# An attention and quantised-linear block on one core: the order of one DMA queue in seven units, the opening tiles, and a few moves beside them

## The reference

```python
xn = (x - mean) / sqrt(var + 1e-5)
# attention: 16 query heads, 8 key/value heads (two query heads share one), head size 16
q, k, v = xn @ Wq.T, xn @ Wk.T, xn @ Wv.T
energy = q @ k.T - abs(i - j) * 2.0 ** -(head + 1)          # ALiBi
att = softmax(energy / sqrt(16)) @ v
attention = att @ Wo.T + bo
# linear: xn quantised per token to int8, int8 weights
x_scale = max(max(abs(xn)), 1e-6) / 127
linear = (round(xn / x_scale) @ weight_q.T) * x_scale * weight_scale + bias
```

## Time and profile before

| | |
|---|---|
| median of three runs | 1568.98 us |
| profiled execution, its own time | 1568.38 us |
| its span, first to last instruction | 1566.4 us |
| granted TensorE clock, mean | 0.992 |
| TensorE matmuls busy | 1497.0 us, 96% |
| VectorE busy | 1394.6 us, 89% |
| ScalarE busy | 1184.8 us, 76% |
| GpSimd busy | 1076.1 us, 69% |
| DMA engines, share over the span on the main queue | 34.2% |

### The profile page before, as it was taken

How to read it: one execution, slowest core, us unless ns; L and a number is a source line. 1 busy time by engine, 2 the same in 40 slices (tenths; PEclk the granted TensorE clock), 3 DMA queues, 4 the chain that set the end, 5 groups by cost and what they waited for, 6 DMA issues and landing times.

```text
span 1566.4 us, 42517 instructions
## 1 busy us (share of the span) xinstructions
PE 1497.0 (96%) x16284; PEld 583.0 (37%) x16284; DVE 1394.6 (89%) x1698; ACT 1184.8 (76%) x2331; POOL 1076.1 (69%) x1627
## 2 busy tenths in 40 slices
PE   5899999999999999999989999999999999999998
PEld 5333333333333333333333334333333333333333
DVE  5999989999899998999979999899998988999981
ACT  3467777777787776887767887777877777788885
POOL 5467777777788876787757877677877776533332
PEclk9999999999999999999999999999999999999999
DMA  6522243333334334333333433433333332312212
GB/s 169 140 76 71 74 100 81 93 98 81 105 83 108 96 79 109 91 92 101 84 92 94 105 85 91 103 98 96 97 83 96 94 92 65 82 49 68 72 44 62
DMA packets 197291, 140.98 MB, mean 90 GB/s; under 512 B 107040, under 2 KB 165728, under 8 KB 197088
## 3 DMA queue, kind: packets, MB, share of 16 engines
q1 hardware_dynamic: 197088, 138.27, 34.2%
HBM read 81.40 MB, written 35.63 MB: 75 GB/s over the span
## 4 chain that ended last, share of the span: by engine, by line
PE 47%; DVE 30%; SPq 9%; issue 8%; DMA 3%; POOL 2%; ACT 0%; POOLq 0%; DVEq 0%; ACTq 0%
DVE row_max L999 27%; PE ps_ring L1279 15%; PE ps_pv L1355 13%; PE ps_row L1296 9%; PE ps_ring L1395 4%; PE ps_ring L1415 3%; SPq L464 2%; SPq L468 2%; SPq L506 2%; DMA q<-neg_max_t 1%; SPq L472 1%; PE ps_ring L1398 1%; DMA k<-k_alibi 1%; DVE pv_turned L1039 1%; PE ps_ring L1409 1%
## 5 line engine op out<-in xcount | busy, mean ns | idle before, releaser
L999 DVE TENSOR_REDUCE row_max<-ps_row 128x1 f32<-128x1024 f32 x1024 | 1199.5, 1213 | 114.7 <-PE ps_row L1298 99.4
L1171 ACT ACTIVATE probs<-ps_ring 128x512 f32<-128x512 f32 x2048 | 1084.5, 601 | 245.2 <-PE ps_ring L1279 242.6
L1279 PE MATMUL ps_ring<-q,k 122*32 122x512 bf16 x8192 | 636.6, 383 | 19.9 <-DMA q<-neg_max_t 19.0
L762 POOL TENSOR_TENSOR probs<-probs,near 128x256 f32<-128x256 f32 x512 | 375.2, 733 | 324.8 <-ACT probs L1171 318.9
L1355 PE MATMUL ps_pv<-probs,v_unit 128*32 128x512 f32 x4096 | 533.5, 596 | 0.0
L1279 PEld LDWEIGHTS ps_ring<-q,k 122*32 122x32 bf16 x8192 | 215.1, 95 | 518.0 <-ACT probs L1171 324.7
L1296 PE MATMUL ps_row<-k,q 64*128 64x512 bf16 x944 | 326.2, 385 | 25.8 <-DVE row_max L999 11.4
L1298 PE MATMUL ps_row<-k_again,q_again 64*128 64x512 bf16 x944 | 326.0, 385 | 0.0
L1296 PEld LDWEIGHTS ps_row<-k,q 64*128 64x128 bf16 x944 | 84.2, 93 | 320.3 <-issue 199.6
L1355 PEld LDWEIGHTS ps_pv<-probs,v_unit 128*32 128x32 f32 x4096 | 124.7, 110 | 54.2 <-issue 7.7
L1298 PEld LDWEIGHTS ps_row<-k_again,q_again 64*128 64x128 bf16 x944 | 84.0, 92 | 0.0
(11 more groups left out here) (84 smaller groups left out, 1012.0 us busy)
## 6 DMA issues: line engine op xcount, KB each, us to landing
parts_dram<-parts SPq DMA_DIRECT2D x59, 288.0 KB, 3.0
q_again<-q SPq DMA_DIRECT2D x63, 256.0 KB, 3.3
token_b<-token_dram SPq DMA_DIRECT2D x53, 256.0 KB, 4.1
q<-parts_dram SPq DMA_DIRECT2D x128, 96.0 KB
k<-parts_dram SPq DMA_DIRECT2D x256, 32.0 KB
q<-parts_dram SPq DMA_DIRECT2D x128, 64.0 KB
att_dram<-att_unit SPq DMA_DIRECT2D x126, 64.0 KB
att_t<-att_dram SPq DMA_DIRECT2D x56, 128.0 KB, 2.9
```

The source lines that it names most:

```text
L762: pool.tensor_tensor(here, here, near[:, u % KV_HEADS, :].rearrange("p (e n) -> p e n", e=GROUP), ALU.mult).then_inc(weighted, 1)
L999: dve.tensor_reduce(row_max[:, par, e, qb:qb + 1], ps_row[qb % 2][:, :], AX_X, ALU.max, negate=True).then_inc(row_max_found, 1)
L1171: act.activation(probs[:, c % PBUFS, e, h * HALF:(h + 1) * HALF], ring_bank(u, c, e, h), ACT.Exp, scale=SCALE).then_inc(ring_freed, 1)
L1279: mm = pe.matmul(to[at, :], weights[:, at], moving, start=start, stop=stop)
```

## The change

On the queue, in the seven units u = 6, 14, ..., 54 (where set u + 2 is late), load_token, place_max, store_att and load_att_t move from the end of the unit's program to its start, the first before and the others behind load_again(u + 2), and so ahead of next_set(u + 3). In the opening stage tiles 0 to 7 are taken through on all engines before tiles 8 to 10, and the largest values of the first eight are found behind their last rest. In units 0 and 1 VectorE's tile work is split over blocks 1 and 3. In even units find_rsum, norm and turn_back change places. The projections of the last sequence are grouped in pairs.

```diff
@@ sync, unit(u, f)
-                if u + 2 < UNITS and late_set(u + 2):
+                copied = u + 2 < UNITS and late_set(u + 2)
+                if copied:
+                    if f["token"]:
+                        load_token(u + 1 + PREP_AHEAD)
                     load_again(u + 2, (u + 2) % SETS)
+                    place_max(u + 1, (u + 1) % SETS)
+                    store_att(u - 1)
+                    for t in f["next_att"]:
+                        load_att_t(t, t % 2)
                 if f["row_set"] and not late_set(u + 3):
                     next_set(u + 3)
...
-                if f["token"]:
-                    load_token(u + 1 + PREP_AHEAD)
-                if not f["last"]:
-                    place_max(u + 1, (u + 1) % SETS)
-                if f["prev"] and u % PAIR == 0:
-                    store_att(u - 1)
-                for t in f["next_att"]:
-                    load_att_t(t, t % 2)
+                if not copied:
+                    if f["token"]:
+                        load_token(u + 1 + PREP_AHEAD)
+                    if not f["last"]:
+                        place_max(u + 1, (u + 1) % SETS)
+                    if f["prev"] and u % PAIR == 0:
+                        store_att(u - 1)
+                    for t in f["next_att"]:
+                        load_att_t(t, t % 2)
@@ gpsimd, opening
-            for t in range(PREP_AHEAD):
-                if t + 4 < PREP_AHEAD:
+            for t in range(BLOCKS):
+                if t + 4 < BLOCKS:
                     find_rstd(t + 4, t % 2)
+                find_low(t, t % 2)
+            for t in range(BLOCKS, PREP_AHEAD):
+                find_rstd(t, t % 2)
+            for t in range(BLOCKS, PREP_AHEAD):
                 find_low(t, t % 2)
@@ gpsimd, unit(u, f)
+                    if c == 4 and f["prev"] and u % PAIR == 0:
+                        norm(u - 1)
                     if c == 4:
                         for made in f["made"][:1]:
                             weigh_linear(made)
...
-                    if c == 3 and f["prev"] and u % PAIR == 0:
-                        norm(u - 1)
@@ vector, opening
             first_stats(2)
-            find_first_largest(0)
             first_stats(3)
-            find_first_largest(1)
-            for t in range(PREP_AHEAD):
-                if t + 2 < PREP_AHEAD:
+            for t in range(BLOCKS):
+                if t + 2 < BLOCKS:
                     normalise(t + 2, t % 2)
-                if t + 4 < PREP_AHEAD:
+                if t + 4 < BLOCKS:
                     first_stats(t + 4)
-                if t + 2 < PREP_AHEAD:
-                    find_first_largest(t + 2)
                 find_rest(t, t % 2, early[t % 2][1])
-                if t == BLOCKS - 2:
-                    find_first_scales(0, BLOCKS, 0)
+            for t in range(BLOCKS, BLOCKS + 2):
+                first_stats(t)
+            for t in range(BLOCKS):
+                find_first_largest(t)
+            find_first_scales(0, BLOCKS, 0)
+            for t in range(BLOCKS, BLOCKS + 2):
+                normalise(t, t % 2)
+            first_stats(PREP_AHEAD - 1)
+            find_rest(BLOCKS, 0, early[0][1])
+            normalise(PREP_AHEAD - 1, 0)
+            for t in range(BLOCKS + 1, PREP_AHEAD):
+                find_rest(t, t % 2, early[t % 2][1])
+            for t in range(BLOCKS, PREP_AHEAD):
+                find_first_largest(t)
             find_first_scales(BLOCKS, PREP_AHEAD, 2)
             dve.wait_ge(w8_loaded, 16)
@@ vector, unit(u, f)
-                at_sums, at_norm = (5, BLOCKS) if apart else (3, 3)
+                at_sums, at_norm = (BLOCKS - 1, SLOTS) if apart else (3, 3)
+                made = 1 if u < PAIR else PAIR
+
+                def here(c):
+                    return slice(0, made) if c == 1 else slice(made, PAIR)
...
-                        if i == SLOTS - 3 and apart:
+                        if i == BLOCKS + 3 and apart:
                             turn_back(u - 1)
-                    if c == 1:
-                        for t in f["normed"]:
+                    if c in (1, 3):
+                        for t in f["normed"][here(c)]:
                             normalise(t, t % 2)
                             find_largest(t, t % 2)
                             find_scale(t, t % 2)
-                        for t in f["stats"]:
+                        for t in f["stats"][here(c)]:
                             wait(dve, x_loaded, 16 * (t - X_AHEAD + 1))
                             find_stats(t, t % 2)
@@ tensor, opening (scalar likewise: tiles 0 to 7, then 8 to 10)
-            for t in range(PREP_AHEAD):
+            for t in range(BLOCKS):
+                make_qk(t, early[t % 2][1])
+                if t + 2 < BLOCKS:
+                    turn_xn(t + 2, early[t % 2][0])
+            for t in range(BLOCKS, BLOCKS + 2):
+                turn_xn(t, early[t % 2][0])
+            for t in range(BLOCKS, PREP_AHEAD):
                 make_qk(t, early[t % 2][1])
                 if t + 2 < PREP_AHEAD:
                     turn_xn(t + 2, early[t % 2][0])
@@ tensor, last sequence
-                slots = i // 2 + (u - UNITS + 2) * BLOCKS - BLOCKS // 2
-                if i % 2 == 0 and 0 <= slots < BLOCKS:
-                    project_last(0, P, slots)
-                if i % 2 == 0 and slots >= BLOCKS + 2:
-                    project_last(1, P - GROUP * HEAD_DIM, slots - BLOCKS - 2)
+
+            def project_pairs(u, c):
+
+                at = (u - UNITS + 2) * BLOCKS + c - BLOCKS // 2
+                if 0 <= at < BLOCKS and at % 2 == 0:
+                    for i in (at, at + 1):
+                        project_last(0, P, i)
+                if u == UNITS - 1 and c in (BLOCKS - 3, BLOCKS - 1):
+                    for i in (c - BLOCKS + 3, c - BLOCKS + 4):
+                        project_last(1, P - GROUP * HEAD_DIM, i)
...
             pv_block(UNITS - 1, (UNITS - 1) % 2, BLOCKS - 2)
-            project_last(1, P - GROUP * HEAD_DIM, 2)
             pv_block(UNITS - 1, (UNITS - 1) % 2, BLOCKS - 1)
-            for i in range(3, BLOCKS):
+            for i in range(BLOCKS // 2, BLOCKS):
                 project_last(1, P - GROUP * HEAD_DIM, i)
```

More of the change, by code:

```diff
@@ L1131, in _ @@
                 keep_xn_t(t, early[t % 2][0])
-            for t in range(PREP_AHEAD):
+            for t in range(BLOCKS):
+                find_high(t, early[t % 2][1])
+                if t + 2 < BLOCKS:
+                    keep_xn_t(t + 2, early[t % 2][0])
+                find_middle(t, t % 2)
+            for t in range(BLOCKS, BLOCKS + 2):
+                keep_xn_t(t, early[t % 2][0])
+            for t in range(BLOCKS, PREP_AHEAD):
                 find_high(t, early[t % 2][1])
@@ L1426, in unit @@
                     ahead_row_block(u, f, 2 * c + 1)
+                    project_pairs(u, c)
                     col_half(u, c, 1, 0)
```

## The result

The changed kernel takes 1600.45 us in the median (1600.42 to 1604.98), the kernel before 1568.74 beside it: ratio 1.0216, interval 1.0187 to 1.0245. It is 32 us slower; I had forecast 13, and a range up to 1596.

A forecast was written before the change was run, and what follows sets the result against it. TensorE's seven waits for the maxima, set by SyncE's queue, were taken as the bound. Queue +11, opening +4, units 0 and 1 -2.4, small moves and closing +0.5: +13.1 on 1568.4 gives 1581.5 us, range 1560 to 1596.

The forecast's parts named there:

- What bounds the kernel: TensorE's weight loads wait for the maxima's DMA at units 7, 15, ..., 55: seven waits, 23.4 us in all.
- part 1: New order on SyncE's queue: removes seven waits (-26 us), new stalls cost 37; net +11, from -12 to +30.
- The events: Seven stretches from the turn of maxima in unit 8k-2 to that in 8k; claimed to cost about 26 us before.
- Where the stall goes: From units 7, 15, ... to the start of units 8, 16, ..., 56; unit 16 starts about 4.7 us late.
- the late set: Rival: copy of set 17 lands after 23, unit 15's second half waits as well; 1590 to 1605 us, chance 8%.
- The sum: Queue's issues and landings from the turn in unit 14, maxima landed at 37.6; later, the whole change's total, +13.1 us.
- five events cost 4.7 + 1.1 = 5.8 each: Starts of five of units 8, 16, ..., 56: 4.7 us of wait plus 1.1 for TensorE's lower clock; 29 together.
- in all 37: New stalls at units 8, 16, ..., 56: five cost 29 us, units 6 to 8 5.3, units 54 to 56 2.7.
- the bounds: New stall at unit 16: 2 us with shorter landings, 8 with the slowest landing and a longer issue.
- Part 2: Opening: tiles 8 to 10 come later, first row maximum at 43 to 47.2 instead of 39.07; +4 us (+1.9 to +6.1).
- Part 3: Units 0 and 1: splitting VectorE's tile work removes TensorE's 1.91 us gap and slow clock; -2.4 us (0 to -3.5).
- Part 4, "at nothing": Small moves of reciprocal, transpose back and GpSimd's multiply are hidden by row maxima, costing nothing; with the closing +0.5 us.

## Why the prediction was right in its sign and wrong in its size

- **What bounds the kernel, and what part 1 removes.** This was right: seven waits, set by the queue. The events cost 345.0 - 321.3 = 23.7 us before, for which I had 26.
- **Where the stall goes.** This was right too: units 8, 16, ..., 56, by way of the copy and of the tokens' trip; the late set hurt nothing else. The sum had the first issue of the maxima 33.7 us behind the turn (35.8 less 2.1); it is 34.9 in the event that I had worked out.
- **"So five events cost 4.7 + 1.1 = 5.8 each" and "in all 37": this step failed, by the sizes of its two terms.** The new stalls cost 374.7 - 321.3 = 53.4.
  - *The wait.* TensorE's waits are 36.9, where my terms make 5 x 4.7 + 4.2 + 1.6 = 29.3. The queue was a microsecond longer than its best known rows. In the event of unit 14 the set lands 5 us after its last issue begins (4.47 taken), the tokens in 4.79 (4.5), and three loads of one line take 0.4 longer; at unit 32 the wait is 8.4.
  - *The clock.* The other 16.5, 2.4 an event, is what follows the waits, for which I had 1.1 each, 7.7 in all. Against 13.50 at full clock, the time from the end of the wait to the next turn is 14.3 longer in sum: this is the clock. The remaining 2.2 I did not take apart. I had let three of seven events speak for waits of 3.3 us, and put them on waits of 5. All seven come back at half clock or fall to it within a microsecond or two, and they pay 1.6 to 2.8 each where 1.4 was my price for one.
- The rule of the Trainium skill that I had weighed there (TensorE: Matmul & The Clock Gate, "HAM oscillation — how this bites in real kernels": matmuls that wait for a DMA come back throttled each time) is what the seven new stalls show. It does not hold of every wait: 2.82 us of idle time, in the run with the maxima ahead of the tokens, left the clock at 1.00. Its count was right here; the sum by it, 2 us higher, still had the price of 1.4.
- **Two readings.** The maxima are wanted at 33.3 behind the turn and not at 32.9, because the first half of an event takes 26.33 and not 25.98; this made five of the seven waits 0.35 shorter. And in the bounds, 28.5 + 2.7 is 31.2, which is 1.8 before 33.0 and not 2.4. Only the lower bound rests on it.
- **Part 2.** The path was right (tiles 8 to 10, their reductions, the cast, tile 11's own steps), and its length between my two cases: the first row maximum came at 45.15, where I had 43 to 47.2. But I let 2 us vanish in gaps, and none did. The first row maximum is 6.1 later than before, the turn in unit 0 6.9. Alone the opening costs 5.8, where 4 was taken; that is within the range of 1.9 to 6.1.
- **Part 3.** It gives -2.1 where -2.4 stood; the gap of 1.91 us is gone.
- **Part 4, "at nothing".** This is true with the queue of the kernel before, and false beside part 1: the earlier transpose back is worth 20 us, because part 1 puts the store in the queue's way. My sum held the store to be ready (2.9 + 2.3), so it had this gain in it without knowing. That was luck; the total is not off by it. The closing costs 1.6 where +0.5 stood and 1.5 was the bound: a projection alone in a block lengthens it by 0.29 us (2.47 against 2.18), and I had not priced what a pair costs (5.07 for a block with and one without, against 4.94); the rest of the 1.6 I did not take apart.
- **The sum.** The measured parts are 29.7 + 6.9 - 2.1 + 1.6 + 0.5, against 11 + 4 - 2.4 + 0.5. Most of the difference is part 1, whose 29.7 stands at the end of its own bounds (-12 to +30).

What the experiments don't settle is how the queue's extra microsecond divides: single issues and landings differ from event to event (the stall of unit 32 is 8.4, that of unit 56 3.0).

## What to carry to other kernels

On one queue a transfer moved ahead of a wait pushes everything else behind it: add up the queue from one deadline to the next, with each landing that an instruction of the queue itself waits for, and look for the place where the next stall comes out. Fill such waits with issues that are due anyway, and split a long train of issues around an urgent one. A stall costs more than its length where TensorE comes back at half clock: neither the share of older, shorter stalls that had it nor their price carried over to longer ones here. And a move that is free by itself can be what another part of the change needs.

## What the runs showed of the hardware

- After a wait of 5.55 us TensorE ran at 0.50 of its clock for some 5 us (windows above); after 2.82 us it came back at 1.00; and in the kernel before three of seven waits, the longest 4.3 us, were followed by the lower clock. The length of the wait alone did not decide it there: after 2.17 us (unit 7) the clock fell to 0.50, after 2.98 us (unit 15) it stayed at 1.00.
- Issues of one and the same kind on SyncE's queue are not of one length: three loads (L472) took 1.34 us in most units, 1.75 in the event of unit 14 of the changed kernel and 2.56 in the same event with the copy behind x.
